# Switched experts in one block: all expert weights loaded at its start, result rows scattered back by token

## The reference, cut to what matters

```python
gates = jax.nn.softmax(xt @ wg, axis=-1)
expert_idx = jnp.argmax(gates, axis=-1)
...
keep = (pos < C).astype(xt.dtype)
gate_val = jnp.sum(gates * mask1, axis=1) * keep
slot = expert_idx.astype(jnp.int32) * C + jnp.clip(pos, 0, C - 1)
disp = jnp.zeros((E * C, M), dtype=xt.dtype).at[slot].add(xt * keep[:, None])
disp = disp.reshape(E, C, M)
h = jax.nn.relu(jnp.einsum('ecm,emh->ech', disp, w1) + b1[:, None, :])
eo = jnp.einsum('ech,ehm->ecm', h, w2) + b2[:, None, :]
out = eo.reshape(E * C, M)[slot] * gate_val[:, None]
```

## Time and profile before

| | us |
|---|---|
| median of 3 runs | 3973.92 (3965.94 to 3974.53) |
| the profiled execution's own time | 3971.7 |
| its span, first to last instruction | 3970.1 |
| PE busy | 3103.3 (78%) |
| DVE busy | 2657.8 (67%) |
| ACT busy | 2192.2 (55%) |
| POOL busy | 293.2 (7%) |
| mean granted clock of PE | 0.881 of full speed |

### The profile page before, as it was taken

How to read it: one execution, slowest core, us unless ns; L and a number is a source line. 1 busy time by engine, 2 the same in 40 slices (tenths; PEclk the granted TensorE clock), 3 DMA queues, 4 the chain that set the end, 5 groups by cost and what they waited for, 6 DMA issues and landing times. The chain is left out here.

```text
span 3970.1 us, 55787 instructions
## 1 busy us (share of the span) xinstructions
PE 3103.3 (78%) x19108; PEld 1256.6 (32%) x19108; DVE 2657.8 (67%) x5332; ACT 2192.2 (55%) x2997; POOL 293.2 (7%) x361
## 2 busy tenths in 40 slices
PE   3899994994699999984999999633359998989433
PEld 2344443442212222223455555511312222222311
DVE  5788864446699999955566666302758888888601
ACT  2366662221267777772455555211459999999311
POOL 2000000000100000000000000033210000000033
PEclk8799996997689999996899999767679999999667
DMA  5423200000532112000000000021252222210022
GB/s 214 71 42 51 47 16 21 0 0 14 159 47 36 33 28 41 15 3 20 9 1 1 1 1 1 1 67 58 101 97 30 33 34 32 35 16 1 3 68 79
DMA packets 158539, 151.67 MB, mean 38 GB/s; under 512 B 46672, under 2 KB 126427, under 8 KB 156000
## 3 DMA queue, kind: packets, MB, share of 16 engines
q1 hardware_dynamic: 152928, 136.30, 16.3%
q0 software_dynamic: 5376, 12.25, 1.0%
HBM read 90.35 MB, written 57.67 MB: 37 GB/s over the span
## 5 line engine op out<-in xcount | busy, mean ns | idle before, releaser
L1029 DVE TENSOR_REDUCE a_part_max<-a_slot_ps 128x1 f32<-128x512 f32 (+3 forms) x1792 | 1007.5, 625 | 78.4 <-PE a_slot_ps L883 53.2
L1013 ACT ACTIVATE a_probs<-a_scores 128x1024 f32<-128x1024 f32 (+3 forms) x896 | 790.4, 933 | 408.3 <-PE a_scores L910 247.6
L1661 DVE TENSOR_TENSOR a_probs<-a_logit_ps,a_gate 128x1024 f32<-128x1024 f32 x512 | 602.5, 1218 | 123.7 <-ACT a_gate L1614 123.6
L883 PE MATMUL a_slot_ps<-a_k_op,a_q_op 48*128 48x512 bf16 (+3 forms) x1792 | 574.2, 380 | 96.1 <-DMA a_k_op<-scratch_k 53.0
L1620 ACT ACTIVATE a_probs<-a_probs 128x1024 f32<-128x1024 f32 x512 | 510.8, 1050 | 0.0
L910 PE MATMUL a_scores<-a_q_op,a_k_op 51*128 51x512 bf16 (+3 forms) x1792 | 469.4, 361 | 7.2 <-ACT a_probs L1013 6.1
L930 PE MATMUL a_o_ps<-a_probs,a_v_op 128*32 128x512 f32 (+3 forms) x3584 | 437.3, 560 | 1.2 <-ACT a_o_sb L1000 0.6
L883 PEld LDWEIGHTS a_slot_ps<-a_k_op,a_q_op 48*128 48x128 bf16 x1792 | 149.9, 94 | 659.7 <-DVE a_part_max L1029 525.5
L1566 PE MATMUL a_logit_ps<-a_q_op,a_k_op 96*128 96x512 bf16 x1024 | 306.1, 387 | 64.2 <-DVE a_probs L1661 57.2
L1614 ACT ACTIVATE a_gate<-a_diff_ps 128x1024 f32<-128x1024 f32 x256 | 261.0, 1020 | 46.3 <-PE a_diff_ps L1566 45.0
L1590 PE MATMUL a_o_ps<-a_probs,a_v_op 128*32 128x512 f32 x2048 | 275.4, 610 | 2.1 <-ACT a_probs L1620 1.5
(11 more groups left out here) (393 smaller groups left out, 3883.4 us busy)
## 6 DMA issues: line engine op xcount, KB each, us to landing
a_q_op<-scratch_q SPq DMA_DIRECT2D x576, 32.0 KB
a_k_op<-scratch_k SPq DMA_DIRECT2D x576, 32.0 KB
scratch_v<-p_vpad SPq DMA_DIRECT2D x16, 1024.0 KB, 4.5
a_v_op<-scratch_v SPq DMA_DIRECT2D x32, 512.0 KB, 6.5
scratch_q<-p_parts SPq DMA_DIRECT2D x24, 384.0 KB, 2.6
scratch_k<-p_parts SPq DMA_DIRECT2D x24, 384.0 KB, 2.6
a_qd_op<-scratch_g SPq DMA_DIRECT2D x192, 32.0 KB
slots<-zero_slots SPq DMA_DIRECT2D x2, 2048.0 KB, 8.6
```

The costliest lines, as they stand in the source:

```text
L883: mm = nc.tensor.matmul(out[:, 0:width], q_op[g][r0:r0 + MAX_ROW, e, qt * P:(qt + 1) * P], k_op[g][r0:r0 + MAX_ROW, e, kh * CH:kh * CH + w ...
L1013: nc.scalar.activation(probs[gs % NB][:, 2 * e:2 * e + 2, off:CH], scores[e][:, :, off:CH], ACT.Exp, scale=scale).then_inc(probs_done, 1)
L1029: nc.vector.tensor_reduce(part_max[u % 2][:, kh, col:col + 1], slot_ps[n % BANKS][:, 0:width_of(s)], axis=AX.X, op=ALU.max).then_inc(slot_ ...
L1661: nc.vector.tensor_tensor(probs[s % 4][m][:], logit_ps[m][:], gate[s % 2][:], op) \
```

## The change

The blocks `dispatch`, `slot_experts`, `combine` and the last store become one block, `switch_experts`. The loop over experts is written out. SP issues the loads of all 8 experts' weights at the block's start, then waits for the sent rows and loads them all. A sent row is 130 floats wide: the token's features, its number (`TOKEN`) and its gate (`GATE`), the last two written by DVE into `xn`. The numbers come from a new constant in HBM (`token_ids`). PE turns the next expert's rows between h and y. The y matmuls have their operands exchanged: 16 matmuls of 128 columns give rows by token, so that nothing is turned back. DVE multiplies by the gate, and POOL scatters the rows by token number into `results` with 4 indirect DMAs per expert; unused slots hold a number out of range. When all have landed, SP loads `results` in 4 plain DMAs, DVE adds each part to `x`, and after layer 3 SP stores each part of `x`. `results` must now be zero beforehand, so the first block fills four HBM tensors instead of two, from two on-chip tiles. `assign_slots` loses `slot_out`. `layer_stats` and `route` address `xn` with a row of 130 instead of 128.

```diff
-            then(nc.vector.tensor_copy(slot_out[:], slot[:]))
...
+ROW = D + 2
+TOKEN, GATE = D, D + 1
...
+def switch_experts(nc, name, x, xn, slot_in, gate, token_ids, slots, returned, w1, w2, biases, ident, stats, out):
...
+        w1_sb, w2_sb = sb("w1_sb", [P, E, HID]), sb("w2_sb", [P, E, FB, D])
+        if biases is not None:
+            b1_sb, b2_sb = sb("b1_sb", [P, E, FB]), sb("b2_sb", [P, E, D])
+            biased = [sb(f"biased{i}", [P, CPT, D]) for i in range(2)]
+        rows = [sb(f"rows{e}", [P, CPT, ROW]) for e in range(E)]
+        dest = [sb(f"dest{e}", [P, CPT], U32) for e in range(E)]
+        rowsT = [sb(f"rowsT{i}", [P, CH]) for i in range(2)]
+        hid = [sb(f"hid{i}", [P, FB, CH]) for i in range(2)]
+        res = [sb(f"res{i}", [P, CPT, D]) for i in range(3)]
+        back = [sb(f"back{b}", [P, KB * D]) for b in range(BATCH)]
+        t_ps = [ps(f"t_ps{i}") for i in range(2)]
+        h_ps = [ps(f"h_ps{f}") for f in range(FB)]
+        y_ps = [ps(f"y_ps{i}") for i in range(2)]
...
+        @block.sync
+        def _(sp):
+            sp.dma_start(ids[:], token_ids).then_inc(ids_loaded, 16)
+            sp.dma_start(w1_sb[:], w1.rearrange("e c f -> c e f")).then_inc(w_loaded, 16)
+            sp.dma_start(w2_sb[:].rearrange("p e n d -> p (e n) d"), w2.rearrange("e (n p) d -> p (e n) d", p=P)).then_inc(w_loaded, 16)
+            if biases is not None:
+                sp.dma_start(b1_sb[:], biases[0].rearrange("e p n -> p e n")).then_inc(w_loaded, 16)
+                sp.dma_start(b2_sb[:], biases[1].to_broadcast([P, E, D])).then_inc(w_loaded, 16)
+            sp.wait_ge(sent, 16 * TILES)
+            for e in range(E):
+                sp.dma_start(rows[e][:], slots[e * CAP:(e + 1) * CAP, :].rearrange("(n p) d -> p n d", p=P)).then_inc(rows_loaded[e], 16)
+            for e in range(E):
+                sp.wait_ge(returned_done[e], 16 * CPT)
+            for b in range(BATCH):
+                sp.dma_start(back[b][:].rearrange("p (n d) -> p n d", d=D),
+                             returned[b * T:(b + 1) * T, :].rearrange("(n p) d -> p n d", p=P)).then_inc(fetched[b], 16)
+            if out is not None:
+                for b in range(BATCH):
+                    sp.wait_ge(added, b + 1)
+                    sp.dma_start(out[b * T:(b + 1) * T, :].rearrange("(n p) d -> p n d", p=P),
+                                 x[:, b * KB * D:(b + 1) * KB * D].rearrange("p (n d) -> p n d", d=D)).then_inc(written, 16)
+                sp.wait_ge(written, 16 * BATCH)
         @block.gpsimd
         def _(pool):
+            pool.wait_ge(marked, 2)
             for t in range(TILES):
                 nc.gpsimd.indirect_dma_start(out=slots, out_offset=bass.IndirectOffsetOnAxis(ap=slot_in[:, t:t + 1], axis=0),
-                                             in_=xn[:, t * D:(t + 1) * D], in_offset=None,
+                                             in_=xn[:, t * ROW:(t + 1) * ROW], in_offset=None,
                                              bounds_check=TOK - 1, oob_is_err=False).then_inc(sent, 16)
-            pool.wait_ge(sent, 16 * TILES)
...
+            for e in range(E):
+                pool.wait_ge(dest_done, e + 1)
+                pool.wait_ge(res_done, e + 1)
+                for t in range(CPT):
+                    nc.gpsimd.indirect_dma_start(out=returned, out_offset=bass.IndirectOffsetOnAxis(ap=dest[e][:, t:t + 1], axis=0),
+                                                 in_=res[e % 3][:, t, :], in_offset=None,
+                                                 bounds_check=TOK - 1, oob_is_err=False).then_inc(returned_done[e], 16)
         @block.tensor
         def _(te):
...
+            def turn(e):
+                te.wait_ge(rows_loaded[e], 16)
+                if e >= 2:
+                    te.wait_ge(turn_copied, e - 1)
+                for t in range(CPT):
+                    mm = nc.tensor.transpose(t_ps[e % 2][:, t * P:(t + 1) * P], rows[e][:, t, 0:D], ident[:])
+                mm.then_inc(turned, 1)
+            turn(0)
+            te.wait_ge(w_loaded, 16 * n_weights)
+            for e in range(E):
+                te.wait_ge(turn_copied, e + 1)
+                for f in range(FB):
+                    if e > 0:
+                        te.wait_ge(h_done, (e - 1) * FB + f + 1)
+                    nc.tensor.matmul(h_ps[f][:], w1_sb[:, e, f * P:(f + 1) * P], rowsT[e % 2][:],
+                                     start=True, stop=True).then_inc(h_ready, 1)
+                if e + 1 < E:
+                    turn(e + 1)
+                te.wait_ge(h_done, (e + 1) * FB)
+                if e >= 2:
+                    te.wait_ge(biased_done if biases is not None else res_done, e - 1)
+                for t in range(CPT):
                     for f in range(FB):
...
+                        mm = nc.tensor.matmul(y_ps[e % 2][:, t * D:(t + 1) * D], hid[e % 2][:, f, t * P:(t + 1) * P],
+                                              w2_sb[:, e, f, :], start=f == 0, stop=f == FB - 1)
+                mm.then_inc(y_ready, 1)
         @block.scalar
         def _(act):
...
+            def take(e):
+                act.wait_ge(turned, e + 1)
+                if e >= 2:
+                    act.wait_ge(h_ready, (e - 1) * FB)
+                nc.scalar.activation(rowsT[e % 2][:], t_ps[e % 2][:], ACT.Copy).then_inc(turn_copied, 1)
+            if biases is not None:
+                act.wait_ge(w_loaded, 16 * n_weights)
+            take(0)
+            for e in range(E):
+                for f in range(FB):
+                    act.wait_ge(h_ready, e * FB + f + 1)
+                    if f == 0 and e >= 2:
+                        act.wait_ge(y_ready, e - 1)
+                    if biases is None:
+                        nc.scalar.activation(hid[e % 2][:, f, :], h_ps[f][:], ACT.Relu).then_inc(h_done, 1)
+                    else:
+                        nc.scalar.activation(hid[e % 2][:, f, :], h_ps[f][:], ACT.Relu, bias=b1_sb[:, e, f:f + 1]).then_inc(h_done, 1)
+                if e + 1 < E:
+                    take(e + 1)
         @block.vector
         def _(dve):
...
+            rows_of = xn[:].rearrange("p (t w) -> p t w", w=ROW)
+            nc.vector.tensor_copy(rows_of[:, :, GATE], gate[:]).then_inc(marked, 1)
+            dve.wait_ge(ids_loaded, 16)
+            nc.vector.tensor_copy(rows_of[:, :, TOKEN], ids[:]).then_inc(marked, 1)
+            for e in range(E):
+                dve.wait_ge(rows_loaded[e], 16)
+                nc.vector.tensor_copy(dest[e][:], rows[e][:, :, TOKEN]).then_inc(dest_done, 1)
+            for e in range(E):
+                weight = rows[e][:, :, GATE:GATE + 1].to_broadcast([P, CPT, D])
+                dve.wait_ge(y_ready, e + 1)
+                fresh = y_ps[e % 2][:].rearrange("p (t d) -> p t d", d=D)
+                if e >= 3:
+                    dve.wait_ge(returned_done[e - 3], 16 * CPT)
+                if biases is not None:
+                    nc.vector.tensor_tensor(biased[e % 2][:], fresh, b2_sb[:, e, :].unsqueeze(1).to_broadcast([P, CPT, D]),
+                                            ALU.add).then_inc(biased_done, 1)
+                    dve.wait_ge(biased_done, e + 1)
+                    fresh = biased[e % 2][:]
+                nc.vector.tensor_tensor(res[e % 3][:], fresh, weight, ALU.mult).then_inc(res_done, 1)
+            for b in range(BATCH):
+                part = x[:, b * KB * D:(b + 1) * KB * D]
+                dve.wait_ge(fetched[b], 16)
+                nc.vector.tensor_tensor(part, part, back[b][:], ALU.add).then_inc(added, 1)
+                if stats is not None:
+                    dve.wait_ge(added, b + 1)
+                    for t in range(b * KB, (b + 1) * KB):
+                        tile_stats(nc, stats, x, t)
...
-        slots = [dram(f"slots{i}", [TOK, D], FP32) for i in range(2)]
+        slots = [dram(f"slots{i}", [TOK, ROW], FP32) for i in range(2)]
...
         with cleared_semaphores(nc):
-            with nc.sbuf_tensor("zero_slots", [P, TILES * D], FP32) as zeros:
+            with nc.sbuf_tensor("zero_slots", [P, TILES * ROW], FP32) as zeros, nc.sbuf_tensor("plain", [P, TILES * D], FP32) as plain:
                 with nc.Block() as block:
                     @block.gpsimd
                     def _(pool):
                         nc.gpsimd.memset(zeros[:], 0.0).then_inc(zeroed, 1)
+                        nc.gpsimd.memset(plain[:], 0.0).then_inc(zeroed, 1)
+                        pool.wait_ge(zeroed, 2)
+                        nc.gpsimd.memset(zeros[:].rearrange("p (n d) -> p n d", d=ROW)[:, :, TOKEN:TOKEN + 1], 2.0 * TOK).then_inc(zeroed, 1)
                     @block.sync
                     def _(sp):
-                        sp.wait_ge(zeroed, 1)
+                        sp.wait_ge(zeroed, 3)
                         for s in slots:
                             sp.dma_start(s.rearrange("(p n) d -> p (n d)", p=P), zeros[:]).then_inc(filled, 16)
+                        for r in results:
```

(35 more changed lines are left out.)

125 lines of the change are left out of this document (22 added, 103 removed).

## The result

The changed kernel takes 3883.8 us, the median of 4 runs (3880.95 to 3886.22), beside 3972.41 for the kernel before: a ratio of 0.9777, interval 0.9764 to 0.979. By medians that is 88.6 less; between the two profiled executions, 3886.22 and 3971.7 themselves, it is 85.5 less. The forecast was 95.7 less.

A forecast was written before the change was run, and what follows sets the result against it. The prediction saw three movable times: the lead into the experts, PE's chain within an expert, and the tail. With the first block's +7.8 its terms summed to -95.7, from 3971.7 to 3876 us; 8-in-10 range 3854 to 3912.

The forecast's parts named there:

- 1, first block and queue: Program start: second memset and two more issues cost 4.6, project's weights queued behind four fills 3.2; together +7.8 us.
- 2, lead, layers 3 and 2: Before the experts: early weights gain 5.9, waiting for token numbers loses 2.1; -3.8 us in each layer.
- 3, experts of layer 3: PE's chain per expert in layer 3: period 7.95 instead of 9.90, first expert 0.6 longer; -13.0 us.
- 3, experts of layer 2: PE's chain per expert in layer 2: period 7.85 instead of 10.07, first expert 0.6 longer; -15.0 us.
- 4, tail of layer 3: Last y to the end: 8.3 to the first load back, then 16.4 of loads and stores; 24.7 against 62.0, -37.3 us.
- 4, tail of layer 2: After layer 2's last y: return, first load, then DVE's adds and statistics without gaps; 22.3 against 52.9, -30.6 us.
- D: Rival: PE stays at 1.2 GHz through the experts, +7.3 per expert, 3993 us, slower than before; chance 0.03.
- the last rival: Last case in the list of chances: nothing measurable changes; chance 0.01.
- C: Rival: more gained, by project's weights passing the fills (-3), loads and stores overlapping (-3), fewer slow PE starts: 3862; chance 0.12.
- A: Rival: y in the experts is bound by its weight loads, 3.1 to 3.4 more each, about 3930 us; chance 0.08.
- B: Rival: POOL's scatter issues hold the experts; at 2.5 per issue period 10.7, +22 per layer, 3920 us; chance 0.08.
- E: Rival: the sends' landing waits for the early weight loads, up to 8 us lost per layer, 3890; chance 0.06.

The follow-up runs named there:

- e7: Changed kernel with results cleared by DVE memsets and stores beside the sends, not in the first block, and b2 loaded ahead of b1: 3874.57 us, ratio 0.9746.
- e6: Changed kernel with token numbers loaded at the program's start and written into xn during the ranking, before the experts' block: 3878.37 us, ratio 0.9764.
- e1: Changed kernel with the expert weights and biases loaded behind the loads of the sent rows, not at the block's start: 3921.27 us, ratio 0.9872.
- e3: Changed kernel with y in its old form, 4 matmuls of 512 columns, nothing turned back, result left wrong: 3878.33 us, ratio 0.976.
- e2: Changed kernel with POOL scattering only after the products of all 8 experts, with 8 result buffers instead of 3: 3949.98 us, ratio 0.9951.
- e8: Changed kernel with e6 and e7 together and the slots filled beside the router, so the first block is gone: 3867.16 us, ratio 0.9734.
- e5: The changed kernel once more, unedited, in the group of e6 to e8 on another chip: 3880.09 us, ratio 0.9767.

## Why the prediction was right, point by point

The mechanism held in each part that was forecast. What missed is sizes, and 6.1 us that I gave nothing. Between the two profiled executions:

| step | forecast | measured | from |
|---|---|---|---|
| 1, first block and queue | +7.8 | +8.3 | 33.48 to 41.74 |
| 2, lead, layers 3 and 2 | -7.6 | -8.7 | -4.2, -4.5 |
| 3, experts of layer 3 | -13.0 | -12.1 | 7 periods -12.9, the first +0.8 |
| 3, experts of layer 2 | -15.0 | -12.6 | 7 periods -14.7, the first +2.1 |
| 4, tail of layer 3 | -37.3 | -36.8 | 62.0 to 25.2 |
| 4, tail of layer 2 | -30.6 | -29.7 | to the next block's first step |
| nothing forecast | 0 | +6.1 | below |
| sum | -95.7 | -85.5 | |

- **The first block** has two errors that nearly cancel. I gave SP's two further issues 0.8; they took 2.20, most likely because the queue held the first two fills (0.90 and 1.26 each, where the first two took 0.33 and 0.43); the first statistics started at 22.7 and not at 21.1. The wait for the weights behind the fills was then 2.3 and not 3.2. That the step came out within 0.5 is partly luck. e7 gives 8.1 for both: the queue model held, with 419 GB/s as in the earlier trace rows.
- **The lead** was priced right in both of its parts: the token numbers cost 1.9 (2.1 forecast, e6), the weights' early issue 6.0 (5.9). e1 shows how much hangs on the second: 38.5 if the new, larger set were loaded late.
- **The experts' period** is 8.05 and 7.96 instead of 7.95 and 7.85. The step that was mis-sized is y: 32 records took 3.68 to the next h, 0.115 each, where I took 3.45, the low half of my own 3.4 to 3.6. e3 puts the price of the narrow form at 0.14. The waiting between h and y was 0.94 (1.0 forecast).
- **The first expert** of layer 2 lost 2.1 instead of 0.6. One us of it is h, which took 6.10 there in place of 5.09 before, and the clock says why: PE has stood idle in the sending for over 50 us in both kernels and starts h at the lower of its two levels, 1.2 GHz, and within h the granted clock rises to 2.4 GHz, but not at one point. Layer 2's first h before and after, then layer 3's:

```profile
2640.30:2645.20 4.90, 4.90 (x8) 2.17 (x9) 0.00 (x0) 1.79 (x3) 0.00 (x0) 0.71 0.00 0
2648.40:2654.30 5.90, 5.90 (x8) 2.47 (x9) 0.85 (x5) 1.79 (x3) 0.00 (x0) 0.59 0.67 181
3829.00:3835.20 6.20, 6.16 (x8) 2.60 (x9) 0.00 (x0) 2.02 (x3) 0.00 (x0) 0.57 0.00 0
3792.30:3798.20 5.90, 5.90 (x10) 2.55 (x11) 1.02 (x6) 2.06 (x3) 0.00 (x0) 0.62 0.72 190
```

 So h lost 1.0 in layer 2 and won 0.5 in layer 3, and what sets the point at which the clock rises is not shown. The rest of the first expert is the same in both layers and was mis-sized: the wait between h and y (0.85 and 0.94, nothing before) and y itself, 0.25 longer to DVE's step, are 1.1 and 1.2 where I took 0.6, although my own period had 1.0 for that wait.
- **The tails**: the sum of loads and stores over one set of DMA engines gave 16.4 for 16.9, and layer 2's adds and statistics ran without gaps as forecast, 2.8 apart, each pair as in the earlier trace rows. e2 confirms that nothing but the 28 covered issues separates the short tail from the long one of the same code.
- **What I gave nothing**: the rows are written with gaps of two columns, and writing them takes 0.8 longer per layer (four turns of 2.40 in place of 2.28, and longer gaps): 1.6. That the gaps are the reason was not tried by itself. The router's weights in layer 2: 1.6, late in seven of the nine kernels with the change, cause open. Layer 0's attention 1.8 and layer 3's 1.1, within what equal code varies by in the runs above.
- **Two slips in the recorded text.** All but D and the last rival is 0.96, not 0.95. And C's two priced terms give 3870; nothing priced the other 8 down to 3862.

**The rivals.** A is excluded by e3 and B by e2 (POOL idle for 3.25 in each expert, waiting for DVE). D did not come: the clock in the experts is 0.95, with the narrow records, where the earlier trace rows have 0.96. E is excluded by the trace of the changed kernel shown under e1. C asked for more than the forecast, and the gain was smaller. The Trainium skill's rule (page TensorE: Matmul & The Clock Gate, section Part 3: Packing small matmuls), by which weight loads of the full array would not overlap matmuls in flight, is contradicted by this case if it is taken alone, as I took it. The same section says further up that a load into the background weight buffer also goes ahead of matmuls in flight; that would fit, but no trace here shows which buffer a load goes to. In the tile below, of the kernel after, records stand 0.115 apart although a load takes 0.19 and a product 0.275 from start to end, so they lie over each other:

```profile
L2278 PEld LDWEIGHTS f3e_y_ps<-f3e_w_sb,f3e_hid x256: 186/192/192, 3798.9 to 3858.8; 128*128 128x128 f32 x128
L2278 PE MATMUL f3e_y_ps<-f3e_w_sb,f3e_hid x256: 275/275/377, 3798.9 to 3858.9; 128*128 128x128 f32 x128
```

## What to carry to other kernels

When an engine's issue rate is the bound of a stage (here 32 indirect DMAs at 1.28), the gain is in starting it as soon as its first data is there: 28 of 32 issues went under the experts and gave 35.7 per layer, with no cost to the engines they ran beside. Look for the wait that holds a closed chain of one engine, too: moving the next tile's turning into the wait for the relu gave 1.4 per expert, where everything else in layer 3's expert together gave 0.46. And what a restructuring adds to a program's first block is paid in full, issue time and the queue behind it; moved beside the sends and the router, the same fills lengthened neither of these stretches, and with the token numbers e8 won 12.9. The new return by itself, with nothing beside it, was 1.2 shorter than the old one in layer 3 and 6.0 longer in layer 2 (e2): its gain is the overlap.

## What the runs showed of the hardware

- An issue on SP's queue is not of one length. The load of b1, in 16-byte pieces, held SP for 11.78. Its small pieces are not the reason: in e7 the issue right behind the two weight loads is the first store of `results`, and that one held SP for 11.09, while b1, issued later, took 1.14. So the long hold comes with the place behind the two weight loads. The issues of project's weights took 0.42 in e8, and 1.26 while the four fills were under way. The long hold lay beside the sends; in e1 it stood on the path.
- POOL's scatters took 0.97 and 0.30 behind it in every case: alone, beside weight loads at a DMA share of 1.03, beside the experts, and beside stores. The fetches of the kernel before took 0.94 and 0.30. Only the issue is so steady: from issue to landing the sends took 2.2 to 2.3 in the kernel before, and up to 6.9 in e5 beside the weight loads (median 2.3) and 8.1 in e8 beside loads and stores (median 5.8).
- Rows of 520 bytes instead of 512 changed no landing on the path (2.8 from the first row load to PE's turning, and 2.2 from the last send to that load), so the doubling that I kept as a bound has no place here.
